# Two attentions: the second half's scores in two pieces, with that half's value rows between them

## The chip, the cores and the metric

One core of a Trainium2 chip. The metric is the device time of one execution in microseconds (us), lower is better. PE is the matmul engine (TensorE), PEld its weight loads, DVE is VectorE, ACT is ScalarE, POOL is GpSimd, SP the engine that issues most DMAs.

## The reference, cut to what matters

A chain of small blocks on x of shape (32, 32, 256): an attention (with a layer norm ahead of it and biases), two gated feed-forward blocks, a second attention (no biases), a linear attention, a paged attention and a mixture of experts. The change touches only the two plain attentions. Each has 16 heads of size 16 over sequences of 32 tokens:

```python
Q, K, V = split_heads(Xn @ Wq + bq), split_heads(Xn @ Wk + bk), split_heads(Xn @ Wv + bv)
scores = jnp.einsum('bhqd,bhkd->bhqk', Q, K) / jnp.sqrt(jnp.float32(D_HEAD))
scores = jnp.where(causal, scores, jnp.float32(-jnp.inf))
A = jax.nn.softmax(scores, axis=-1)
AV = jnp.einsum('bhqk,bhkd->bhqd', A, V)
return AV.swapaxes(-2, -3).reshape(X.shape[:-1] + (D_MODEL,)) @ Wo + bo
```

The second attention scales q by a temperature of its sequence and has no biases; otherwise it is the same.

## The kernel before, in words

Both attentions are one class, `Attention`, called as `att_a` and `att_b` (L1817, L1818). Every engine runs its own list of instructions in the order in which the code writes them; semaphores order the engines against each other, through `wait(engine, name, count)` and `then_inc`. There is no planner: the order of the calls is the schedule.

The 1024 tokens are 8 tiles of 128 (four sequences each), in two halves of four tiles. The 256 features are two chunks (c) of 128. PSUM, where matmuls write, has eight banks, `ps[:, 0..7]`.

PE (`tensor`, L358 to L440), in this order: keys of the first half into banks 0 and 1, queries into 2 and 3 (`project`, L361), value rows of the first half into banks 4 and 5 (`value_rows`, L368, 16 matmuls), then `scores(0)` into banks 0 to 3 (L377): 256 matmuls of 32x32 by 32x64. Then the second half's keys into banks 6 and 7, its queries into 4 and 5, its value rows into 6 and 7 (after `k_kept_late`), and `scores(1)` into banks 4 to 7, which therefore waits until the queries (`q_kept`) and the values (`v_kept`) have been copied out. After the wait for `scaled` 4 (DVE has read all first-half scores) come the weighted sums, `weigh(g)` for the 8 tiles in banks 0 and 1 (L397), with the output projections `out_rows` in banks 2 and 3 (L407) between them.

DVE (`vector`, L442): keys of the first half to SBUF (L450 or L453), the values (`keep_values`, L465 with bias, L469 without), and for each tile `up_to_exponent` (L480 scales and masks the scores out of PSUM, L485 takes the maximum), `sums` (L491, L493) and `turn` (L497, transposes the probabilities). ACT (`scalar`, L532): queries (L538), second-half keys (L545), `exponent` (L552), `place` (L560, three copies of a quarter into a block-diagonal tile), `keep_output` (L565). POOL (`gpsimd`, L590): subtracts the maximum (L599), multiplies by the reciprocal sum (L604), places the last quarter (L612).

For one tile the data goes PE, DVE, POOL, ACT, DVE, POOL, DVE, ACT and POOL, PE. In DVE's list the second half begins at `if g == 4` (L515): `keep_values(2)`, `keep_values(3)`, `sums(3)`, `turn(2)`, `up_to_exponent(4)`. In ACT's list `exponent(4)` stands ahead of `keep_output(0)` and `place(2)`.

Of the kernel before, what the change touches and what calls it, by code (L numbers as in the profile page):

```python
# [33 lines left out]
B, S, D = 32, 32, 256  # L34
T = B * S
KC = D // P
# [175 lines left out]
def program(nc, small_at, x_tok_d, x_feat_d, mix_table, small_d, ints_d, wA_d, wB_d, wF_d, wG_d, wL_d, wP_d,  # L212
# [7 lines left out]
    with ExitStack() as ctx:  # L220
# [87 lines left out]
        def split_buf(name, base, at, cols):  # L308
# [19 lines left out]
              for name, at in (("z_hi", 6656), ("z_lo", 0))]  # L328
# [4 lines left out]
                         max_done=NT, shifted=NT, exp_done=NT, sum_done=NT, rec_done=NT, normed=NT, turned=NT, placed=3 * NT,  # L333
                         placed_last=NT, pv_done=NT, o_kept=NT, proj_done=4, out=4)

        class Attention:


# [12 lines left out]
            def s(self, name):  # L351
                return sem("att_" + name)
# [5 lines left out]
            def tensor(self, pe):  # L358
                s, inp = self.s, self.inp

                def project(w, n, banks, done):  # L361
                    for c in range(KC):
                        for k in range(KC):
                            mm = nc.tensor.matmul(ps[:, banks[c], :], w[:, k, c * P:(c + 1) * P],
                                                  inp[:, k, n * HALF:(n + 1) * HALF], start=(k == 0), stop=(k == KC - 1))
                        mm.then_inc(s(done), 1)

                def value_rows(n):  # L368
                    for g in range(4 * n, 4 * n + 4):
                        for k in range(KC):  # L370
                            mm = nc.tensor.matmul(ps[:, 4 + g // 2, (g % 2) * D:(g % 2 + 1) * D],
                                                  inp[:, k, g * P:(g + 1) * P], self.wv[:, k, :],
                                                  start=(k == 0), stop=(k == KC - 1))
                        if g % 2:
                            mm.then_inc(s("v_done"), 1)

                def scores(n):  # L377
                    for g4 in range(4):
                        for c in range(KC):
                            for pr in range(4):  # L380
                                for j in range(4):
                                    t0 = (4 * (4 * n + g4) + j) * S
                                    mm = nc.tensor.matmul(
                                        ps[32 * j:32 * j + 32, 4 * n + pr, (2 * g4 + c) * 64:(2 * g4 + c + 1) * 64],
                                        qT[32 * pr:32 * pr + 32, c, t0:t0 + S], kpar[32 * pr:32 * pr + 32, c, :, t0:t0 + S],
                                        start=True, stop=True)
                    mm.then_inc(s("scores_done"), 1)

                def weigh(g):
                    self.wait(pe, "placed", 3 * (g + 1))  # L390
                    self.wait(pe, "placed_last", g + 1)
                    if g >= 2:
                        self.wait(pe, "o_kept", g - 1)
                    for c in range(KC):
                        for pr in range(4):
                            for a in range(2):
                                mm = nc.tensor.matmul(ps[32 * pr:32 * pr + 32, g % 2, c * P:(c + 1) * P],  # L397
                                                      vpar[:, g, a, 4 * c + pr, :], pdiag[:, g % 2, 4 * pr + 2 * c + a, :],
                                                      start=(a == 0), stop=(a == 1))
                    mm.then_inc(s("pv_done"), 1)  # L400

                def out_rows(n, c):
                    self.wait(pe, "o_kept", 4 * (n + 1))
                    if n:
                        self.wait(pe, "out", c + 1)
                    for k in range(KC):
                        mm = nc.tensor.matmul(ps[:, 2 + c, :], self.wo[:, k, c * P:(c + 1) * P],  # L407
                                              attT[:, k, n * HALF:(n + 1) * HALF], start=(k == 0), stop=(k == KC - 1))
                    mm.then_inc(s("proj_done"), 1)

                pe.wait_ge(sem(self.load[0]), self.load[1])
                pe.wait_ge(sem(self.in_ready[0]), self.in_ready[1] + 2)
                project(self.wk, 0, (0, 1), "k_done")
                if self.second_input:
                    self.second_input()
                pe.wait_ge(sem(self.in_ready[0]), self.in_ready[1] + 4)
                project(self.wq, 0, (2, 3), "q_done")
                value_rows(0)
                self.wait(pe, "k_kept", 4)
                self.wait(pe, "q_kept", 2)  # L420
                scores(0)
                project(self.wk, 1, (6, 7), "k_done")
                self.wait(pe, "v_kept", 4)
                project(self.wq, 1, (4, 5), "q_done")
                self.wait(pe, "k_kept_late", 4)
                value_rows(1)
                self.wait(pe, "q_kept", 4)
                self.wait(pe, "v_kept", 8)
                scores(1)
                self.wait(pe, "scaled", 4)  # L430
                for g in range(4):
                    weigh(g)
                weigh(4)
                out_rows(0, 0)
                weigh(5)
                out_rows(0, 1)
                weigh(6)
                weigh(7)
                out_rows(1, 0)
                out_rows(1, 1)  # L440

            def vector(self, dve):  # L442
# [14 lines left out]

                def keep_values(i):
                    self.wait(dve, "v_done", i + 1)
                    v = ps[:, 4 + i, :].rearrange("p (g h a d) -> p g h a d", g=2, h=8, a=2)  # L460
                    bv = const("bv").rearrange("p (h a d) -> p h a d", h=8, a=2)
                    for a in range(2):
                        if self.biased:
                            for g in range(2):
                                ins = nc.vector.tensor_tensor(vpar[:, 2 * i + g, a, :, a * HD:(a + 1) * HD],  # L465
                                                              v[:, g, :, a, :], bv[:, :, a, :], ALU.add)
                            ins.then_inc(s("v_kept"), 1)
                        else:
                            nc.vector.tensor_copy(vpar[:, 2 * i:2 * i + 2, a, :, a * HD:(a + 1) * HD],  # L469
                                                  v[:, :, :, a, :]).then_inc(s("v_kept"), 1)  # L470
# [42 lines left out]
                keep_values(1)  # L513
                for g in range(NT + 1):
                    if g == 4:  # L515
                        keep_values(2)
                        keep_values(3)
                        sums(3)
                        turn(2)
                        up_to_exponent(4)  # L520
                        continue
                    if g < NT:
# [1599 lines left out]
```

## Time and profile before

| | |
|---|---|
| three runs | 604.6 us median (602.22, 604.6, 605.16) |
| profiled execution | 608.92 us, its span 607.0 us, mean granted clock 0.882 |
| PE busy | 500.5 us (82%) |
| PE weight loads | 365.2 us (60%) |
| DVE busy | 374.6 us (62%) |
| ACT busy | 235.9 us (39%) |
| POOL busy | 262.3 us (43%) |
| the first attention | about 19 to 84 us of the span |
| the second attention | about 268 to 323 us of the span |

The span runs from the first to the last instruction of one execution. A row of a timeline shows when a run of equal instructions started, how long the run took, and in brackets how long the engine had been idle before it and what ended that; "issue" there is idle time with no cause in the profile. A busy share is an average over stages with different limits, so the stretches around the two score groups have to be read by themselves.

### The profile page before, as it was taken

The numbers are of one execution on the slowest core, as the hardware profiler recorded it, in microseconds if no ns is written. First come the engines' busy times: TensorE is split into PE (matmuls) and PEld (weight loads), VectorE is DVE, ScalarE is ACT, GpSimd is POOL, SyncE is SP. The second block draws the span as 40 slices with busy tenths as digits, with TensorE's granted clock in tenths as the row PEclk, the third lists the DMA queues.
The fourth block names the chain that finished last, engine by engine and source line by source line (L and its number), as shares of the span: only waits on it lengthen the run. The fifth ranks groups of instructions, "written<-read, shape, count | busy, mean of one in ns | idle before, by whom it ended". The sixth has DMA issues, their size and how long they took to land. (4 is left out here: it accounts for less than half of the span.)

```text
span 607.0 us, 10570 instructions
## 1 busy us (share of the span) xinstructions
PE 500.5 (82%) x4069; PEld 365.2 (60%) x4069; DVE 374.6 (62%) x784; ACT 235.9 (39%) x510; POOL 262.3 (43%) x240
## 2 busy tenths in 40 slices
PE   2968699999999999999687599739999894079966
PEld 0545457887687788766553254626776484069956
DVE  3645757887687788855654764976888356124421
ACT  6125855344342443233581001545666241024430
POOL 5023833464353577774550000278860104616650
PEclk9879699999999999999879759958999776569987
DMA  4991027000000122230001919411100001298416
GB/s 164 384 411 50 1 85 188 0 1 1 1 0 1 35 62 60 65 110 3 2 2 35 207 36 351 168 35 27 27 19 2 2 1 44 96 335 274 139 57 206
DMA packets 25969, 55.95 MB, mean 92 GB/s; under 512 B 4744, under 2 KB 17185, under 8 KB 25024
## 3 DMA queue, kind: packets, MB, share of 16 engines
q1 hardware_dynamic: 19952, 45.06, 22.3%
q0 software_dynamic: 5968, 10.22, 5.6%
q8 instruction: 33, 0.54, 0.4%
q14 instruction: 16, 0.13, 0.1%
HBM read 44.24 MB, written 12.37 MB: 93 GB/s over the span
## 5 line engine op out<-in xcount | busy, mean ns | idle before, releaser
L697 PE MATMUL ps<-x_split,gate_up_split 128*128 128x512 f32 x384 | 96.3, 393 | 0.1
L697 PEld LDWEIGHTS ps<-x_split,gate_up_split 128*128 128x128 f32 x384 | 72.0, 188 | 17.1 <-issue 1.4
L1859 POOL DMA_INDIRECT wbig<-new_kv,prepi x40 | 43.4, 1086 | 86.5 <-DMA new_kv<-work 75.4
L890 POOL TENSOR_TENSOR gate_up_split<-wbig,gate_up_split 128x768 fp32r<-128x768 f32 (+1 forms) x24 | 41.6, 1734 | 52.0 <-ACT gate_up_split L830 51.9
L812 DVE TENSOR_TENSOR hidden_split<-work,hidden_split 128x512 fp32r<-128x512 f32 x34 | 37.7, 1110 | 23.1 <-ACT hidden_split L879 23.1
L879 ACT ACTIVATE hidden_split<-work 128x512 fp32r<-128x512 f32 x34 | 21.4, 630 | 61.4 <-DVE work L807 59.2
L721 PE MATMUL ps<-hidden_split,down_split 128*128 128x512 f32 x160 | 42.5, 395 | 3.0 <-issue 1.4
L1804 POOL DMA_INDIRECT chosen<-work,wbig x31 | 30.5, 985 | 29.7 <-issue 15.0
L896 POOL TENSOR_TENSOR down_split<-wbig,down_split 128x384 fp32r<-128x384 f32 (+1 forms) x24 | 29.1, 1214 | 26.2 <-ACT down_split L837 26.1
L599 POOL TENSOR_TENSOR work<-work,prep 128x512 f32<-128x512 f32 x16 | 16.8, 1048 | 53.5 <-DVE prep L485 52.8
L1859 POOL DMA_INDIRECT wbig<-in_cache_dram,prepi x32 | 33.5, 1047 | 7.6 <-issue 6.6
L721 PEld LDWEIGHTS ps<-hidden_split,down_split 128*128 128x128 f32 x160 | 29.8, 188 | 11.0 <-issue 4.6
L1513 ACT ACTIVATE wmid<-ps,prep 128x160 f32<-128x160 f32 x64 | 24.6, 390 | 22.1 <-DVE prep L1412 22.1
L397 PE MATMUL ps<-work 128*32 128x128 f32 x512 | 23.8, 349 | 9.3 <-ACT work L560 9.3
L1801 POOL DMA_INDIRECT sorted<-work,prepi x16 | 16.2, 1013 | 35.1 <-DVE prepi L1671 30.5
L807 DVE TENSOR_TENSOR work<-ps,work 128x512 f32<-128x512 f32 x34 | 23.2, 683 | 12.1 <-PE ps L702 8.5
L560 ACT ACTIVATE work<-work 32x512 f32<-32x512 f32 x48 | 29.9, 624 | 0.9
L872 ACT ACTIVATE work<-ps 128x512 f32<-128x512 f32 x34 | 20.2, 594 | 25.3 <-PE ps L702 13.3
L1707 PE MATMUL ps<-small,wbig 128*128 128x128 f32 x62 | 12.4, 287 | 20.5 <-DMA wbig<-sorted 20.5
L397 PEld LDWEIGHTS ps<-work 128*32 128x32 f32 x512 | 19.0, 136 | 16.1 <-ACT work L560 15.6
L1330 PE MATMUL ps<-work 128*128 128x160 f32 x128 | 27.8, 343 | 0.0
L1782 ACT ACTIVATE work<-ps 128x128 f32<-128x128 f32 x31 | 8.6, 278 | 46.9 <-PE ps L1718 46.9
(321 smaller groups left out, 1162.8 us busy)
## 6 DMA issues: line engine op xcount, KB each, us to landing
work<-in_wE_dram SPq DMA_DIRECT2D x1, 5376.0 KB, 16.1
wbig<-in_wF_dram SPq DMA_DIRECT2D x1, 4992.0 KB, 21.4
work<-work SPq DMA_DIRECT2D x32, 128.0 KB, 2.4
sorted<-wmid SPq DMA_DIRECT2D x1, 3999.0 KB, 15.8
wbig<-in_wG_dram SPq DMA_DIRECT2D x1, 3072.0 KB, 28.2
wbig<-in_wE_dram SPq DMA_DIRECT2D x6, 384.0 KB, 3.8
wbig<-chosen SPq DMA_DIRECT2D x8, 256.0 KB, 5.1
wbig<-sorted SPq DMA_DIRECT2D x1, 1935.0 KB, 13.2
```

The lines of the kernel that those rows point to most:

```text
L397: mm = nc.tensor.matmul(ps[32 * pr:32 * pr + 32, g % 2, c * P:(c + 1) * P], vpar[:, g, a, 4 * c + pr, :], pdiag[:, g % 2, 4 * pr + 2 * c + ...
L560: nc.scalar.activation(pdiag[q, g % 2, :, q], scor[q, g % 4, :].rearrange("p (h k) -> p h k", h=NH), ACT.Copy).then_inc(s("placed"), 1)
L697: mm = nc.tensor.matmul(o, self.gus[:, w % 2, a, 2 * m + k, :], self.xs[:, b, k, n * HALF:(n + 1) * HALF], start=(k == 0 and a == b), stop ...
L721: nc.tensor.matmul(o, self.dns[:, w % 2, a, c], hs[:, i % 2, 0, :], start=(p == 0 and a == 0), stop=False)
L807: nc.vector.tensor_tensor(hid[:, i % 3, :], ps[:, 5 + 2 * (i % 2), :], gated[:, i % 2, :], ALU.mult).then_inc(s("h_ready"), 1)
L812: nc.vector.tensor_tensor(hs[:, i % 2, 1, :], hid[:, i % 3, :], hs[:, i % 2, 0, :].bitcast(F32), ALU.subtract).then_inc(s("h_lo"), 1)
L890: nc.gpsimd.tensor_tensor(self.gus[:, k % 2, 1, 0:self.gu_chunks], self.gate_up[:, :, j * P:(j + 1) * P], self.gus[:, k % 2, 0, 0:self.gu_ ...
L896: nc.gpsimd.tensor_tensor(self.dns[:, k % 2, 1, 0:self.dn_cols], self.down[:, j, :], self.dns[:, k % 2, 0, 0:self.dn_cols].bitcast(F32), A ...
L1330: mm = nc.tensor.matmul(ps[:, 2 + b % 2, a * NKEY:(a + 1) * NKEY], qmask[:, b, 2 * a:2 * a + 2, :, :].rearrange("p g h t -> p (g h t)"), k ...
L1513: nc.scalar.activation(pex[:, b % 3, a, :], ps[:, 2 + b % 2, a * NKEY:(a + 1) * NKEY], ACT.Exp, bias=pst[:, b, a:a + 1], accum_out=pst[:, ...
L1804: send(chosen_d, by(tile_x(t)[:, D + 1:ROW]), y_tile[:, t % 8, :], None, bounds_check=2 * T - 1, oob_is_err=False)\
L1859: return nc.gpsimd.indirect_dma_start(dst, None, table, bass.IndirectOffsetOnAxis(ap=rows.bitcast(U32), axis=0), **({} if bound is None el ...
```

## The change

`value_rows` takes its bank from a tuple: 4 and 5 for the first half as before, 2 and 3 for the second half instead of 6 and 7. `scores` can do one of the two feature chunks alone. On PE the second half's scores of chunk 0 come first, then the wait for `scaled` 4, the value rows, and the scores of chunk 1, which signal `scores_done`. The wait for `v_kept` 8 moves to after the fourth `weigh`. On DVE `sums(3)` and `turn(2)` go ahead of `keep_values(2)` and `keep_values(3)`. The number of instructions stays the same on each engine.

```diff
--- before.py
+++ after.py
@@ -333,6 +333,8 @@
                          max_done=NT, shifted=NT, exp_done=NT, sum_done=NT, rec_done=NT, normed=NT, turned=NT, placed=3 * NT,
                          placed_last=NT, pv_done=NT, o_kept=NT, proj_done=4, out=4)
 
+        VALUE_BANK = (4, 5, 2, 3)
+
         class Attention:
 
 
@@ -368,15 +370,15 @@
                 def value_rows(n):
                     for g in range(4 * n, 4 * n + 4):
                         for k in range(KC):
-                            mm = nc.tensor.matmul(ps[:, 4 + g // 2, (g % 2) * D:(g % 2 + 1) * D],
+                            mm = nc.tensor.matmul(ps[:, VALUE_BANK[g // 2], (g % 2) * D:(g % 2 + 1) * D],
                                                   inp[:, k, g * P:(g + 1) * P], self.wv[:, k, :],
                                                   start=(k == 0), stop=(k == KC - 1))
                         if g % 2:
                             mm.then_inc(s("v_done"), 1)
 
-                def scores(n):
+                def scores(n, chunks=range(KC)):
                     for g4 in range(4):
-                        for c in range(KC):
+                        for c in chunks:
                             for pr in range(4):
                                 for j in range(4):
                                     t0 = (4 * (4 * n + g4) + j) * S
@@ -384,7 +386,8 @@
                                         ps[32 * j:32 * j + 32, 4 * n + pr, (2 * g4 + c) * 64:(2 * g4 + c + 1) * 64],
                                         qT[32 * pr:32 * pr + 32, c, t0:t0 + S], kpar[32 * pr:32 * pr + 32, c, :, t0:t0 + S],
                                         start=True, stop=True)
-                    mm.then_inc(s("scores_done"), 1)
+                    if KC - 1 in chunks:
+                        mm.then_inc(s("scores_done"), 1)
 
                 def weigh(g):
                     self.wait(pe, "placed", 3 * (g + 1))
@@ -423,13 +426,14 @@
                 self.wait(pe, "v_kept", 4)
                 project(self.wq, 1, (4, 5), "q_done")
                 self.wait(pe, "k_kept_late", 4)
+                self.wait(pe, "q_kept", 4)
+                scores(1, (0,))
+                self.wait(pe, "scaled", 4)
                 value_rows(1)
-                self.wait(pe, "q_kept", 4)
-                self.wait(pe, "v_kept", 8)
-                scores(1)
-                self.wait(pe, "scaled", 4)
+                scores(1, (1,))
                 for g in range(4):
                     weigh(g)
+                self.wait(pe, "v_kept", 8)
                 weigh(4)
                 out_rows(0, 0)
                 weigh(5)
@@ -457,7 +461,7 @@
 
                 def keep_values(i):
                     self.wait(dve, "v_done", i + 1)
-                    v = ps[:, 4 + i, :].rearrange("p (g h a d) -> p g h a d", g=2, h=8, a=2)
+                    v = ps[:, VALUE_BANK[i], :].rearrange("p (g h a d) -> p g h a d", g=2, h=8, a=2)
                     bv = const("bv").rearrange("p (h a d) -> p h a d", h=8, a=2)
                     for a in range(2):
                         if self.biased:
@@ -513,10 +517,10 @@
                 keep_values(1)
                 for g in range(NT + 1):
                     if g == 4:
+                        sums(3)
+                        turn(2)
                         keep_values(2)
                         keep_values(3)
-                        sums(3)
-                        turn(2)
                         up_to_exponent(4)
                         continue
                     if g < NT:
```

## Rows read from the trace of the kernel before

**Rows 1.** Timeline, PE, first attention: start us, length us, engine, line, names, count [idle before]
```profile
29.04 3.62 PE L371 MATMUL ps<-wmid,work 128*128 128x256 f32 x16
...
32.59 2.50 PE L383 MATMUL ps<-work 32*32 32x64 f32 x237
...
39.70 0.48 PE L383 MATMUL ps<-work 32*32 32x64 f32 x19 [4.60 <-issue]
...
49.90 3.62 PE L371 MATMUL ps<-wmid,work 128*128 128x256 f32 x16
...
54.58 2.18 PE L383 MATMUL ps<-work 32*32 32x64 f32 x205 [1.06 <-DVE work L465]
...
58.55 0.74 PE L383 MATMUL ps<-work 32*32 32x64 f32 x51 [1.78 <-issue]
```

**Rows 2.** Timeline, DVE and ACT, first attention, around the second half's scores
```profile
47.39 0.65 DVE L480 SCALAR_TENSOR_TENSOR work<-ps,small 128x512 f32<-128x512 f32 x1
...
50.10 0.69 ACT L538 ACTIVATE work<-ps,small 128x512 f32<-128x512 f32 x1 [0.89 <-PE ps L364]
...
53.55 0.88 DVE L465 TENSOR_TENSOR work<-ps,small 128x128 f32<-128x128 f32 x4 [0.84 <-PE ps L371]
54.35 0.67 DVE L491 TENSOR_REDUCE prep<-work 128x16 f32<-128x512 f32 x1
...
55.23 0.65 DVE L497 STREAM_TRANSPOSE work<-work 128x512 f32<-128x512 f32 x1
...
59.33 0.69 DVE L480 SCALAR_TENSOR_TENSOR work<-ps,small 128x512 f32<-128x512 f32 x1 [3.44 <-PE ps L383]
```

**Rows 3.** Timeline, PE, second attention
```profile
278.72 2.71 PE L383 MATMUL ps<-work 32*32 32x64 f32 x256
...
288.33 3.62 PE L371 MATMUL ps<-wmid,xT 128*128 128x256 f32 x16
292.89 2.46 PE L383 MATMUL ps<-work 32*32 32x64 f32 x233 [0.94 <-DVE work L469]
297.18 0.37 PE L383 MATMUL ps<-work 32*32 32x64 f32 x23 [1.83 <-issue]
```

**Rows 4.** Timelines of DVE and of ACT, second attention
```profile
288.47 0.71 DVE L480 SCALAR_TENSOR_TENSOR work<-ps,prep,small 128x512 f32<-128x512 f32 x1
...
297.69 0.75 DVE L480 SCALAR_TENSOR_TENSOR work<-ps,prep,small 128x512 f32<-128x512 f32 x1 [3.49 <-PE ps L383]
...
288.80 1.07 ACT L538 ACTIVATE work<-ps 128x512 f32<-128x512 f32 x2
```

**Rows 5.** Timeline of ACT, first attention, exponent of tile 4
```profile
61.97 0.63 ACT L552 ACTIVATE work<-work 128x512 f32<-128x512 f32 x1 [6.89 <-POOL work L599]
```

**Rows 6.** Windows: stretch, length, busy us of each engine, granted clock, DMA share, GB/s
```profile
32.50:40.20 7.70, 3.10 (x258) 2.65 (x257) 0.88 (x4) 0.00 (x0) 0.00 (x0) 0.92 0.98 417
66.40:76.50 10.10, 7.99 (x77) 4.55 (x80) 6.53 (x13) 8.73 (x16) 7.12 (x9) 0.50 0.00 0
```

**Rows 7.** The page: busy us and instructions by engine; DMA queues (packets, MB, share)
```profile
PE 500.5 (82%) x4069; PEld 365.2 (60%) x4069; DVE 374.6 (62%) x784; ACT 235.9 (39%) x510; POOL 262.3 (43%) x240
...
q8 instruction: 33, 0.54, 0.4%
```

**Rows 8.** DMA in windows (40 slices each): 54.5:59.3, then 292.8:297.6, then 50:54.5
```profile
GB/s 0 0 0 0 0 0 0 0 0 0 0 0 0 137 0 0 0 0 0 0 0 0 0 0 0 0 0 0 0 0 0 0 0 0 0 0 0 0 0 0
...
GB/s 0 0 0 0 0 0 0 0 0 0 0 0 0 0 0 0 137 0 0 0 0 0 0 0 0 0 0 0 0 0 0 0 0 0 0 0 0 0 0 0
...
DMA packets 0, 0.00 MB, mean 0 GB/s; under 512 B 0, under 2 KB 0, under 8 KB 0
```

**Rows 9.** Timeline, PE: output projections, two of the first attention, one of the second
```profile
72.36 3.78 PE L407 MATMUL ps<-work,wmid 128*128 128x512 f32 x4
...
77.33 1.98 PE L407 MATMUL ps<-work,wmid 128*128 128x512 f32 x4
...
310.77 2.61 PE L407 MATMUL ps<-work,wmid 128*128 128x512 f32 x4
```

## The prediction

> **What bounds the kernel now.** I read the page first: in a span of 607.0 us PE is the busiest engine with 500.5 [rows 7], but the two attentions are stretches in which it stands still between bursts. So the timeline of each attention comes next, then the waits of the instructions around the scores, then the DMA of those few microseconds, and last the granted clock.
>
> In both attentions the second half's scores end late. In the first attention PE does the value rows from 49.90, waits until DVE has copied them out (53.55 + 0.88 = 54.43), and starts the 256 score matmuls at 54.58. It gets 205 of them out by 56.8, stands still, resumes at 58.55 and ends at 59.29 [rows 1]. DVE takes the first score tile at 59.33 after 3.44 us of idleness [rows 2]. The second attention repeats it: value rows from 288.33, 0.94 us idle until DVE's copies, scores from 292.89, 233 matmuls, a stop until 297.18, DVE on at 297.69 [rows 3, 4]. After that come shift (POOL), exponent and placing (ACT), weighted sum (PE). ACT's exponent of tile 4 waits 6.89 us for POOL, which waits for DVE [rows 5]; from there on ACT is nearly full (8.73 of 10.1 us [rows 6]) and sets the pace of the tiles, so what the scores end later, the attention ends later, one for one.
>
> The stop inside the scores is no wait of the program; the rows call it "issue". I take it for instruction fetch. The instruction queue q8 moved 33 packets, 0.54 MB in all, 16 KB each [rows 7]. PE has 4069 matmuls and as many weight loads, about 8430 instructions with its waits, so 33 packets hold 256 each, 128 pairs of matmul and weight load. The places fit: from the stop after 237 pairs of the first scores to the stop after 205 of the second are 19 + 16 + 16 + 205 = 256 pairs, two packets. And within each stop's window the only packet on any queue is one of q8 (the one packet of the rows, 0.02 MB): 13 slices of 0.12 us into 54.5 to 59.3, so at 56.1, and 16 slices into 292.8 to 297.6, so at 294.7 [rows 8]. Runs of 237 and 51 pairs take 2.50 and 0.74 us [rows 1], so 9.5 ns a pair and 0.25 us for the last one's own length: a packet is used up in 1.2 us. The packet before the stop's place is entered 77 pairs into the scores (54.58 + 0.73 = 55.3) and the next one can run at 58.55: 3.2 us. The second attention gives 105 pairs, 293.9, to 297.18: 3.3 us. So with 3.3 us between two such borders nothing stops.
>
> **The change part by part.** Times are those of the profiled run (608.92 us, of which the span is 607.0; the median of the runs shown is 604.6, 4.3 lower, and I take differences over to it unscaled).
>
> *Order on PE.* New: wait for q_kept, 128 score pairs (chunk 0), wait for scaled, 16 value matmuls, 128 score pairs (chunk 1). No instruction is added or taken away.
>
> First attention: the last query chunk leaves ACT at 50.10 + 0.69 = 50.79 [rows 2]. Releasing PE took 0.15 before (54.43 to 54.58), so 50.94. 128 pairs at 9.5 ns: 52.15. Value rows take 3.55 from their first matmul to the first score (29.04 to 32.59) [rows 1]: 55.70. 128 pairs and the last one's 0.25: 57.16. DVE begins 0.04 later, 57.20 instead of 59.33: **2.1 us**.
>
> Second: queries leave ACT at 288.80 + 1.07 = 289.87, PE 290.01, then 291.22, 294.77, 296.23; DVE 0.14 later (as 297.55 to 297.69), 296.37 instead of 297.69 [rows 4]: **1.3 us**. It gains less since ACT gives the queries later, 1.5 us behind the value rows' old start.
>
> *Why the stop goes.* The borders lie 93 pairs into the first piece and 77 into the second (121 and 105 in the second attention). Between them are 35 + 77 pairs and the value rows: 1.1 + 3.55 = 4.6 us, over the 3.3 needed, 1.3 to spare. The spare could be eaten by other transfers: the first scores of the first attention, with DMA 98% busy at 417 GB/s, stopped for 4.60 us [rows 1, 6]. From 50 to 54.5, where the first piece will ask for its packet, no packet of any kind moved [rows 8], so I take no delay. Bounds: 0 to 1.3 of stop again in the first attention.
>
> *The new wait, scaled 4,* stands ahead of value rows and behind it are they, the second piece and the weighted sums. DVE finished that read at 47.39 + 0.65 = 48.04, 4.1 us before PE comes at 52.15 [rows 2]; in the second attention at 288.47 + 0.71 = 289.18, 2.0 us before 291.22 [rows 4]. Nothing.
>
> *DVE's order.* sums(3) and turn(2) go ahead of the copies. They took DVE 1.53 us, 54.35 to 55.88, the moment it was free [rows 2], and can now begin earlier. The two pairs of copies take 0.88 each, and the last follows the last value row at 55.70, so DVE is done at 56.6 while PE does the second piece to 57.16. At worst sums begins no earlier than before: 55.88, 56.76, 57.64, and DVE's tile is 0.4 late. I take 0, since the value it waits for is an exponent issued long before; bound 0 to 0.4 in each. PE's wait for v_kept comes after four weighted sums, far later.
>
> *Banks 2 and 3.* They held the first scores, free after scaled 4; out_rows uses them after v_kept 8. No new wait.
>
> *Two more changes of matmul shape in each attention.* Scores start at 32.59, while the value rows' last ends at 29.04 + 3.62 = 32.66 [rows 1]: a switch shows nothing. I take 0. Upper bound: one score matmul's length, 0.25, for each of four switches, 1.0 us in all; nothing could make a switch a gain.
> The Trainium skill (TensorEngine Tiling (Array Packing), Key Properties) says that a change of tiling mode drains the engine. It gives no price; by it the sum would lose something at each switch, and the row above doesn't show it.
>
> *Granted clock.* The tail of the first attention ran at a granted clock of 0.50 (1.2 GHz) from 66.4 to 76.5, behind weighted sums with gaps between them, and so four projection matmuls took 3.78 us against 1.98 right behind; in the second attention the same four took 2.61 [rows 6, 9]. The tails differ by where the fall ends, which the change moves. Worth for each tail: minus 1.8 to plus 1.8 us. I take 0, since the bursts behind the scores keep their spacing, and the fall comes with them.
>
> Sum: 2.1 + 1.3 = 3.4 us, 604.6 - 3.4 = **601.2 us**. What is late next is the query copy on ACT (PE idle 0.7 and 1.4 us ahead of the first piece) and then the chain of DVE, POOL and ACT. Everything later in the kernel starts behind the attentions; the loads of the next weights are landed or triggered by that work, so the gain should reach the end.
>
> **Rivals.**
> *A, the stop stays.* If the stop isn't fetch but belongs to a run of small matmuls, or comes back in the second piece, 2.0 us return in each attention (58.55 less 54.58 + 1.95): 3.4 - 4.0 = -0.6, 605.2 us. For it: the rows name no cause. Against: 256 score pairs ran from 278.72 in 2.71 us without a stop [rows 3], and the places fit borders of 256 instructions. Had 12 pairs moved them to one side, a border lies nearly at that run's start, so its fetch was ahead.
> The Trainium skill (Runtime: NRT & Kernel Launch, Instruction fetch mechanics) has the same 16 KiB blocks of 256 instructions, but calls their cost mostly hidden and gives PE room for 2048 instructions. By that no stop would be fetch, and A would hold; the trace shows a packet of q8 inside the stops, and disagrees.
>
> *B, the clock takes it back.* PE now idles before the first piece and the whole second half comes elsewhere against the clock. If the second attention's tail runs at half clock as the first one's did (3.78 against its 2.61 for four matmuls, 1.2 us, and as much again on the sums and projections behind them) 2.4 us are lost: 603.6 us. For it: two attentions with the same code show two tails. Against: it can as well go the other way.
>
> *C, the other side: each piece stops at its own border.* Every piece contains one border. If a packet is asked for only when PE gets near it, and not while the value rows are waited for, both pieces stop for 2.0 us: -0.6 - 4.0 = -4.6, 609.2 us, slower. It decides where the fetch takes longer than the time between borders, that is above 4.6 us; the stop of 4.60 us at 35 to 39.7 under heavy loads shows that such a time occurs. Against: from 50 on nothing is loading.
>
> **How the numbers follow.** Forecast 0.64, A 0.15, B 0.14, C 0.07. The forecast's own range is 599.0 to 602.8 (clock tails, shape switches 1.0, DVE cover). The range that holds 8 in 10 must reach into A: 598.6 to 605.6. I count over 0.5% (3.0 us, below 601.6) as faster, about what can be told from no change: the forecast lies only 0.4 beyond, so of its 0.64 two thirds are faster, 0.43, and 0.01 of B; slower are C and 0.02 of B, where both tails lose, 0.09; same is the rest, 0.47.
>
> **What would show it.** In the changed kernel's timeline: score matmuls in runs of 128 with no "issue" stop; the first piece right behind ACT's second L538; DVE's first L480 of the second half 6.4 us after the last queries leave ACT in the first attention (57.2 - 50.8) and 6.5 in the second (296.4 - 289.9); q8 packets still one per 256 PE instructions. Wrong if a stop of about 2 us stands in either piece (A, C), if DVE's L465 ends after the last score, if scaled holds PE, or if the gain is there at 60 us and at 300 us but not at the end (B, or a load that waits for nothing of this).

## The result: slower by 0.9%, and the profile after

The changed kernel took 609.4 us (median of 6 runs, 607.33 to 610.49) against 603.6 us (median of 6); the ratio is 1.0093, 95% interval 1.0064 to 1.0122, so 5.6 us slower where 601.2 was forecast. One of the six runs of the kernel before, at 695.58 us, was in a slow state and is left out of the ratio. On another chip the ratio was 1.0119 (1.0075 to 1.0163).

The profiled execution of the changed kernel (607.33 us, span 605.5) was the fastest of its six; that of the kernel before (608.92 us) lay above the 601.5 to 605.2 of its other timed runs. Their spans can't be set against each other; stretches of them can. The timeline of PE, first attention after the change (answers to [rows 1]):

```profile
29.68 3.62 PE L373 MATMUL ps<-wmid,work 128*128 128x256 f32 x16
33.23 2.51 PE L385 MATMUL ps<-work 32*32 32x64 f32 x237
40.71 0.48 PE L385 MATMUL ps<-work 32*32 32x64 f32 x19 [4.97 <-issue]
41.12 8.52 PE L366 MATMUL ps<-work,wmid 128*128 128x512 f32 x16
50.51 1.12 PE L385 MATMUL ps<-work 32*32 32x64 f32 x93 [0.87 <-ACT work L542]
53.81 0.61 PE L385 MATMUL ps<-work 32*32 32x64 f32 x35 [2.18 <-issue]
54.35 5.31 PE L373 MATMUL ps<-wmid,work 128*128 128x256 f32 x16
59.59 1.48 PE L385 MATMUL ps<-work 32*32 32x64 f32 x128
```

and the second (to [rows 3]):

```profile
280.38 2.71 PE L385 MATMUL ps<-work 32*32 32x64 f32 x256
283.03 7.13 PE L366 MATMUL ps<-xT,wmid 128*128 128x512 f32 x16
291.67 1.40 PE L385 MATMUL ps<-work 32*32 32x64 f32 x120 [1.51 <-ACT work L542]
295.64 0.43 PE L385 MATMUL ps<-work 32*32 32x64 f32 x8 [2.57 <-issue]
296.01 5.65 PE L373 MATMUL ps<-wmid,xT 128*128 128x256 f32 x16
301.59 1.47 PE L385 MATMUL ps<-work 32*32 32x64 f32 x128
```

The stop has left the second piece and now stands in the first, at 93 and 120 pairs, the places that the prediction gave for the border there. And the value rows behind it take 5.3 and 5.65 us, not 3.62. DVE, around the second piece (to [rows 2] and [rows 4]):

```profile
59.70 0.89 DVE L469 TENSOR_TENSOR work<-ps,small 128x128 f32<-128x128 f32 x4 [0.84 <-PE ps L373]
61.10 0.69 DVE L484 SCALAR_TENSOR_TENSOR work<-ps,small 128x512 f32<-128x512 f32 x1 [0.52 <-PE ps L385]
```
```profile
301.70 0.76 DVE L473 COPY work<-ps 128x256 f32<-128x256 f32 x2 [1.11 <-PE ps L373]
303.10 0.75 DVE L484 SCALAR_TENSOR_TENSOR work<-ps,prep,small 128x512 f32<-128x512 f32 x1 [0.65 <-PE ps L385]
```

The copies end before the last score, and DVE then waits for PE, as forecast. The windows over the stops and over the value rows (columns as in [rows 6]):

```profile
52.00:53.80 1.80, 0.00 (x0) 0.00 (x0) 0.90 (x3) 1.75 (x4) 0.54 (x1) 1.00 0.00 0
54.40:59.60 5.20, 5.20 (x19) 4.06 (x18) 0.89 (x5) 0.26 (x1) 0.00 (x0) 0.69 0.01 3
293.10:295.60 2.50, 0.00 (x0) 0.00 (x0) 1.51 (x3) 2.43 (x5) 1.28 (x2) 0.50 0.02 7
296.00:301.60 5.60, 5.60 (x22) 4.35 (x18) 0.76 (x2) 0.00 (x0) 0.00 (x0) 0.65 0.01 3
```

PE does nothing in the stops, and the value rows get a mean granted clock of 0.69 and 0.65, a mix of the two levels, 1.2 and 2.4 GHz. The two stops differ: in the first attention the clock is still full during the stop (1.00) and falls behind it, in the second it is at half (0.50) from the stop's start.

Where did the packet come? DMA from 41.5 to 49 us before the change, then after it; then 50 to 54 after it:

```profile
DMA packets 471, 2.34 MB, mean 312 GB/s; under 512 B 192, under 2 KB 192, under 8 KB 320
## 3 DMA queue, kind: packets, MB, share of 16 engines
q1 hardware_dynamic: 470, 2.33, 75.8%
q8 instruction: 1, 0.02, 0.9%
```
```profile
DMA packets 469, 2.30 MB, mean 307 GB/s; under 512 B 192, under 2 KB 192, under 8 KB 320
## 3 DMA queue, kind: packets, MB, share of 16 engines
q1 hardware_dynamic: 469, 2.30, 74.6%
...
GB/s 0 0 0 0 0 0 0 0 0 0 0 0 0 0 164 0 0 0 0 0 0 0 0 0 0 0 0 0 0 0 0 0 0 0 0 0 0 0 0 0
```

Before, one packet of q8 came while PE did the second half's projections (the trace has it at 43.5). After, none did; it came in slice 14 of 0.1 us from 50, at 51.5, 1.0 us after q_kept released PE at 50.45. In the second attention it moved from 284.7 (PE in the query projection) to 293.25, 1.6 us after the release at 291.6. So the packet that the first piece needs started late, with nothing else on the DMA queues.

### The profile page after: what moved, and what is told of

The parts are those of the page before. It is cut to its first block and busy times, and to the rows that moved or that the text cites. A ratio compares the mean times of both kernels' runs of the same rounds, so it can differ in the third digit from the quotient of the medians.

```text
span 605.5 us, 10572 instructions
## 1 busy us (share of the span) xinstructions
PE 498.0 (82%) x4069; PEld 365.1 (60%) x4069; DVE 375.3 (62%) x784; ACT 235.8 (39%) x510; POOL 262.3 (43%) x240
## 5 line engine op out<-in xcount | busy, mean ns | idle before, releaser
L894 POOL TENSOR_TENSOR gate_up_split<-wbig,gate_up_split 128x768 fp32r<-128x768 f32 (+1 forms) x24 | 41.5, 1732 | 51.9 <-ACT gate_up_split L834 51.8
L400 PE MATMUL ps<-work 128*32 128x128 f32 x512 | 20.7, 315 | 12.4 <-ACT work L564 12.4
L400 PEld LDWEIGHTS ps<-work 128*32 128x32 f32 x512 | 16.7, 124 | 19.2 <-ACT work L564 16.1
```

What stands on the lines that cost most here:

```text
L894: nc.gpsimd.tensor_tensor(self.gus[:, k % 2, 1, 0:self.gu_chunks], self.gate_up[:, :, j * P:(j + 1) * P], self.gus[:, k % 2, 0, 0:self.gu_ ...
```

## The experiments

The chips of the groups differ (the kernel before took 618.2, 617.6, 602.5 and 603.3 us there), so ratios to the kernel before on the same chip are compared. "Theory F" is the late fetch: a packet of instructions that is asked for too late. A pair is one weight load and its matmul, and a wait record is an instruction that does nothing but wait.

The instruction stream shows what could hold the request. Where PE waits for two semaphores in a row, the first is carried by the next weight load, and the other becomes a wait record of its own ahead of it. Before the change k_kept_late was carried by the value rows' first weight load. After it, k_kept_late and q_kept stand together, and the trace has a wait record on q_kept at 50.4 and at 291.6 us (`wait` is a helper, L358, so its records have that line; windows 40:60 and 285:300):

```profile
L358 PEldq EVENT_SEMAPHORE  x1: 51/51/51, 50.4 to 50.4; - x1
L358 PEldq EVENT_SEMAPHORE  x1: 51/51/51, 291.6 to 291.6; - x1
```

**e1: one wait.**
```diff
-                self.wait(pe, "k_kept_late", 4)
                 self.wait(pe, "q_kept", 4)
                 scores(1, (0,))
```


> The changed kernel without PE's wait for k_kept_late 4 ahead of the first piece (q_kept 4, which ACT signals later in its order, stays). Theory F (late fetch): of two waits in a row one becomes a wait record of its own in PE's instruction stream, and while PE's sequencer stands in it, behind the first scores, the request for the next instruction packet doesn't go out; the packets come at 51.6 and 293.35 us of the changed trace, 1.1 and 1.7 us behind the release by q_kept. With one wait, carried by the first weight load, the sequencer goes on: packets as early as before the change (43.5 and 284.7 there), no stop at 93 and 120 pairs, value rows at full clock (3.6 us, not 5.3 and 5.65). Time: changed kernel 609.4 less 2 x 2.4 (stops) less 2 x 1.8 (clock) = 601.0. Rival S (spacing: two dense pieces are too close behind the first scores for the fetch, whatever the waits): both stops stay at 2 to 3 us, 609.4. Rival K (the loss is made by the clock alone): the stops stay or go without moving the time by more than 1 us.

Ratio 0.9947 (0.9914 to 0.9980), where 601.0 us, that is 0.9957, was expected. PE in the second series (e1_again):

```profile
50.33 1.48 PE L385 MATMUL ps<-work 32*32 32x64 f32 x128 [0.78 <-ACT work L541]
51.74 3.72 PE L373 MATMUL ps<-wmid,work 128*128 128x256 f32 x16
55.39 1.48 PE L385 MATMUL ps<-work 32*32 32x64 f32 x128
...
286.14 1.48 PE L385 MATMUL ps<-work 32*32 32x64 f32 x128 [1.42 <-ACT work L541]
287.54 3.72 PE L373 MATMUL ps<-wmid,xT 128*128 128x256 f32 x16
291.19 1.48 PE L385 MATMUL ps<-work 32*32 32x64 f32 x128
```

Whole pieces, no stop, value rows at full clock. The packets came at 45.6 and 282.4 in e1_one_wait, while PE did the projections. S and K are out: same matmuls, same spacing, one wait record less in each attention, no stops, and 1.5% between this and the changed kernel. The two ratios are from different chips; on one chip, below, the changed kernel (1.0119) and two versions without its stops in the second halves (e6 0.9993, e7 0.9978) are 1.3 and 1.4% apart.

**e2: the two waits in the other order.**
```diff
-                self.wait(pe, "k_kept_late", 4)
                 self.wait(pe, "q_kept", 4)
+                self.wait(pe, "k_kept_late", 4)
                 scores(1, (0,))
```


> The changed kernel with the two waits ahead of the first piece in the other order, so that the wait of its own is k_kept_late (released at 47.8 us in the first attention, about 289.3 in the second) and q_kept (50.4 and 291.5) is carried by the weight load. Theory F: the packets are asked for some 1.1 to 1.7 us behind the release of the wait of its own, so they move from 51.6 to about 49.2 and from 293.35 to about 290.7, and each stop shrinks from 2.2 and 2.6 us to 0 to 0.7; time 601 to 604. Rival S: nothing changes, 609.4, since the instructions and their number are the same.

0.9915 (0.9883 to 0.9947). The packets came at 49.18 and 285.60, each 1.1 to 1.2 us behind the end of ACT's second-half keys (48.05 and 284.36), the release of the wait record; no stop, the first pieces 1.70 and 1.59 us long instead of 1.48. (This profile reaches the second attention's first scores 4.9 us earlier than the changed kernel's, 275.4 against 280.4, so 285.6 stands for the 290.7 expected.) The packet follows the wait record.

**e3: the kernel before, with q_kept's wait moved ahead of the value rows.**
```diff
                 self.wait(pe, "k_kept_late", 4)
-                value_rows(1)
                 self.wait(pe, "q_kept", 4)
+                value_rows(1)
```


> The kernel before with one line moved: PE waits for q_kept 4 together with k_kept_late 4 ahead of the value rows; nothing is split, banks as before. Theory F: the packets that came at 43.5 and 284.7 come 1.1 to 1.7 us behind q_kept's release, at about 52 and 291.5, and the value rows begin 0.9 and 1.5 us later; the stops inside the scores keep their place (205 and 233 pairs), and a further stop at 77 and 105 pairs comes only if packet plus 2.2 us is later than that: 54.2 against 56.2, so none. Time 603.6 + 2.4 = 606.0 or less. Rival S: packets where they were, time 606 as well; the packets' times tell the two apart, not the total.

1.0047 (1.0013 to 1.0080), 2.9 us. The packets came at 54.2 and 294.3, 1.0 and 1.6 us behind the record's release (53.17 and 292.68), and the stops kept their places (205 and 233 pairs). So without any split the same wait record holds the packet back. DMA of e3 from 44 to 56 us, slices of 0.3:
```profile
GB/s 382 437 437 367 389 447 391 393 468 262 151 117 113 44 56 26 0 0 0 0 0 0 0 0 0 0 0 0 0 0 0 0 0 0 55 0 0 0 0 0
```

**e4: borders moved by 20 pairs.** `for j in [0] * (10 if g == 0 else 0) + list(range(4)):` in the first gather's matmuls.

> The changed kernel with ten surplus 32x32 matmuls (20 pairs of matmul and weight load, 40 instructions) behind the first gather, where PE waits for the next gather anyway; they write again what is written there. If the stops are borders of instruction packets of 256, all stops move 20 pairs ahead: the first scores' from 237 to 217 pairs, the first pieces' from 93 to 73 and from 120 to 100. If they belong to runs of small matmuls or to the data, they stay at 237, 93 and 120. The time may change little: 609 plus up to 1.

PE in e4:
```profile
37.96 2.34 PE L385 MATMUL ps<-work 32*32 32x64 f32 x217
...
55.45 1.47 PE L385 MATMUL ps<-work 32*32 32x64 f32 x128 [0.87 <-ACT work L542]
...
294.40 1.19 PE L385 MATMUL ps<-work 32*32 32x64 f32 x100 [0.78 <-ACT work L542]
297.72 0.39 PE L385 MATMUL ps<-work 32*32 32x64 f32 x28 [2.14 <-issue]
```
237 became 217 and 120 became 100: the stops are borders of the stream. The one expected at 73 didn't come. Its packet came at 47.0 us. I read that so: with the border 40 instructions earlier, it had been asked for before the sequencer reached the wait record. That I had not foreseen. In the second attention the borders moved by 40 instructions too, and there the packet was late all the same, at 295.39, 1.05 us after the record's release at 294.34. The second attention's first scores, free of stops before, stopped at 245 pairs. Ratio 1.0132 of two runs; the surplus matmuls at the start weren't hidden as expected (the second key block starts at 30.87, in the other profiles at 25.5 to 28.2), so its total says nothing.

**after_again: the changed kernel beside the next three.**

> The changed kernel unaltered, on the chip of this group, so that the others can be set against it. If theory F holds in all: first pieces of 93 and 120 pairs, a stop, value rows of 5.3 to 5.7 us, and a ratio to the kernel before near 1.009. If the ratio of 1.009 came from anything outside the attentions, it may be elsewhere here.

1.0119; 93 and 120 pairs, stops of 2.17 and 2.30 us, value rows of 5.41 and 5.85. The packets came 1.04 and 1.16 us after the record's release.

**e5: no split.** Banks 2 and 3, DVE's new order and the late v_kept wait kept, `scores(1)` whole behind the value rows.

> The changed banks and the later v_kept wait alone: value rows of the second half in banks 2 and 3 (after scaled 4) first, then all 256 score pairs in one piece (q_kept carried, k_kept_late as the wait of its own). The scores needn't wait for the copies of the values: PE goes on at 49.90 + 3.55 = 53.45 instead of 54.58, and at 291.88 instead of 292.89, 2.1 us in all; the stops at 205 and 233 pairs stay, 2.0 us each. Time: before less 2.1 us, ratio 0.9965. If the value of the split is that the fetch gets time between borders, this stays behind the split kernels of one wait (0.9947 and 0.9915) by the stops less the wait for the queries, about 1.3 us. If it is as fast or faster, the split brought nothing.

0.9973 (0.9956 to 0.9991), 1.7 us faster than before where 2.1 were expected. Stops of 1.91 and 1.92 us at 205 and 232 pairs. Against the split without its stops (0.9947 and 0.9915 in the group before, 0.9981, 0.9963 and 0.9971 below) the difference is not resolved: no total here shows that the split itself gains anything over e5. e5 too has a wait record (on k_kept_late, at 50.5 and 288.7), but its value rows stand between the border and the record, and its packets came before it, at 44.8 and 284.0.

**e6: DVE's old order on e1.**

> The changed kernel without the k_kept_late wait (as e1_one_wait) and with DVE's old order: keep_values(2), keep_values(3), sums(3), turn(2). The last copies can't begin before the last value row, and sums and turn (1.5 us) now follow them, while the second score piece takes 1.5: DVE reaches the second half's first tile about 1.0 us late in each attention. Expected ratio to the kernel before 0.9947 + 0.0033 = 0.998. If DVE's order is worth nothing, 0.995 as e1.

0.9993 (0.9965 to 1.0021), where e1 had 0.9947 (on another chip; 0.9981 and 0.9963 later, so the totals don't resolve it). DVE in e6, then in e1_again:
```profile
56.35 0.89 DVE L468 TENSOR_TENSOR work<-ps,small 128x128 f32<-128x128 f32 x4 [0.84 <-PE ps L373]
57.15 0.68 DVE L494 TENSOR_REDUCE prep<-work 128x16 f32<-128x512 f32 x1
57.87 0.25 DVE L496 RECIPROCAL prep<-prep 128x16 f32<-128x16 f32 x1
58.03 0.65 DVE L500 STREAM_TRANSPOSE work<-work 128x512 f32<-128x512 f32 x1
58.61 0.65 DVE L483 SCALAR_TENSOR_TENSOR work<-ps,small 128x512 f32<-128x512 f32 x1
```
```profile
55.49 0.88 DVE L468 TENSOR_TENSOR work<-ps,small 128x128 f32<-128x128 f32 x4 [0.40 <-PE ps L373]
56.90 0.69 DVE L483 SCALAR_TENSOR_TENSOR work<-ps,small 128x512 f32<-128x512 f32 x1 [0.52 <-PE ps L385]
```
In e6 DVE goes straight from the transposition to the scores and starts 0.9 us after the last one (56.24 + 1.47 = 57.71); in e1 it waits for PE. In the second attention e6's DVE starts 0.75 us after the last score (298.20 against 297.45), e1_again's 0.04. The new order is worth 0.9 and 0.7 us at this place.

**e7: the first attention's first half split too, on e2.** `scores(0, (0,))`, `value_rows(0)`, `scores(0, (1,))`.

> The version of e2_waits_swapped with the first half of the first attention split too: chunk 0 of scores(0), value rows, chunk 1. There the stop is 4.4 to 5.3 us, since the fetch takes about 6 us from border to resumption while weights are loading. Borders then lie 125 pairs into the first piece and 109 into the second, 4.6 us apart: the stop shrinks to about 1.5 us. PE waits about 1.1 us for q_kept 2 ahead. Expected 2 to 2.5 us less than e2, ratio 0.987 to 0.989. If the stop there belongs to something else that ends at a fixed time (the weight loads), nothing is gained, or 1 us lost.

0.9978 (0.9951 to 1.0005), no gain where 0.987 to 0.989 was expected. The first piece stopped for 2.85 us at 125 pairs and the value rows took 6.24 at a mean granted clock of 0.58. Its packet came at 32.8, 3.6 us after the release of the wait record on k_kept (29.2), under full DMA load. I read it as the same mistake made anew, but did not try it without the record, and the load alone may have made the packet late. In the second half of that attention e7 has e2's two waits and a wait record released at 49.6, but the packet came at 46.15, ahead of it. The instructions are the same there; what differs is that PE had passed the border before it without a stop (e2 stopped there for 4.42 us). So a record so close behind a border does not always hold the packet.

**e8: value rows in two pieces as well.** PE's list (`value_rows` takes the tiles as an argument):
```diff
-                self.wait(pe, "k_kept_late", 4)
-                self.wait(pe, "q_kept", 4)
-                scores(1, (0,))
                 self.wait(pe, "scaled", 4)
-                value_rows(1)
+                value_rows(1, (4, 5))
+                self.wait(pe, "q_kept", 4)
+                scores(1, (0,))
+                value_rows(1, (6, 7))
                 scores(1, (1,))
```


> The changed kernel with the value rows in two pieces as well: 8 value matmuls (tiles 4 and 5, behind scaled 4) ahead of the first score piece, 8 behind it, and k_kept_late's wait dropped, so that no wait record of its own is left. PE fills the wait for the queries: first attention 49.9, 51.7, first piece to 52.9, values to 54.7, second piece to 56.2, against 57.2 before; second attention 289.3 (scaled), 291.1, 292.3, 294.1, 295.6 against 296.2. The borders are 1.22 + 1.78 = 3.0 us apart where 3.3 are needed: a stop of about 0.3 us in each second piece. Sum about 1 us less than e1 and e2, ratio 0.993. Rival: with less than 3.3 us between borders the stops and the clock behind them come back in full (2 us and more each), and it is slower than e1.

1.0008 (0.9991 to 1.0026); and once more:

> e8_values_in_halves once more. Its attentions took 55.2 and 53.9 us in the first profile, 5.8 us less together than the profile of the kernel before, yet its time was that of the kernel before (ratio 1.0008). If the gain within the attentions is real but its total was a matter of that chip or of the clock behind, the ratio here is nearer to 0.995; if something later always gives it back, it is 1.001 again.

0.9992 (0.9969 to 1.0015). The second pieces took 1.62 and 1.52 us (1.72 and 1.53 in the repeat), so the stops were at most 0.2. From the first value row to the last score it took 6.8 us in each attention where 6.3 was expected; the time was that of the kernel before all the same.

**e1 and e2 repeated.**

> e1_one_wait once more, to be set against e2_again and e8 on one chip. Theory F: no stops in the second half's scores, so its ratio lies where the first forecast had the change, 3.4 us under the kernel before, 0.9945.

> e2_waits_swapped once more. Its instructions and e1's differ by one wait record, and both ran without a stop, so they should be equal, near 0.9945; the 0.9915 of the first group was then in part the clock's phase. If the swapped order is really better, it repeats 0.9915.

> e1_one_wait a third time (0.9947, 0.9981 so far). Theory F with the tails' clock phase: the ratio lies between 0.994 and 0.999, without stops; attentions of 55.4 to 56.7 and 55.4 to 57.1 us.

e1: 0.9981 (0.9941 to 1.0022) and 0.9963 (0.9923 to 1.0002). e2: 0.9971 (0.9934 to 1.0008). In e2_again's second attention the value rows took 5.41 us without any stop ahead:

```profile
287.00 1.59 PE L385 MATMUL ps<-work 32*32 32x64 f32 x128 [1.42 <-ACT work L542]
288.52 5.41 PE L373 MATMUL ps<-wmid,xT 128*128 128x256 f32 x16
```
```profile
288.50:293.80 5.30, 5.30 (x23) 4.14 (x16) 2.26 (x5) 2.66 (x5) 1.30 (x2) 0.68 0.01 3
```

PE had idled 1.42 us for the queries, and the clock fell 1.7 us after the piece's start. Without a stop ahead the second attention's value rows were slow in two more profiles, e6 (5.41) and e7 (5.22), each behind 1.42 or 1.43 us of idle time, and at 3.72 in the other four (e1 three times, e2), behind the same idle time. In the changed kernel's second attention the clock fell 1.4 us after the piece's start, at 293.1, when the stop had only begun: that fall is not shown to be the stop's doing. In the first attention all eight profiles without a stop in the first piece have value rows of 3.72 us, and the two with one 5.31 and 5.41. e1's twelve runs of that group lie in two bunches: five at 596.96 to 597.19 us with a mean granted clock of 0.90, and five at 604.6 to 605.8 with 0.886 to 0.889.

**Profiles of the kernel before.**

> The kernel before once more, for a second profile. From its first key projection of the second block (L364) to the feed-forward block's first matmul the first attention took 59.8 us, the second 55.1 from its first matmul to the linear attention's. Theory T (the tails' clock phase moves a single attention by up to 1.8 us either way): here 58 to 61 and 54 to 57, the difference lying behind the scores. If both repeat within 0.3 us, what e1 lacks in the second attention (55.4 against 55.1) is the edit's own doing.

The expectation of the third said the same. From the second key block (L364) to the feed-forward block's first matmul, and from the second attention's first matmul to the linear attention's, in us, each from one profile:

```
kernel             first    second   both
before             59.8     55.1     114.9
before, 2nd        58.45    56.9     115.3
before, 3rd        58.4     56.5     114.9
changed            60.8     60.3     121.1
changed, again     61.0     58.7     119.7
e1 (three)    55.9 55.4 55.0   55.4 55.4 53.85   111.3 110.8 108.9
e2 (two)           55.5 56.7    55.5 57.1        111.0 113.8
e8 (two)           55.2 57.4    53.9 54.0        109.1 111.4
```

One attention of the unchanged kernel varies by 1.4 to 1.8 us with the clock of its tail (its four output projections took 2.61, 3.67 and 3.78 us in the second attention). The changed kernel's two are 5.4 us above the mean of before (120.4 against 115.0), nearly all of the 5.6 that the runs show.

The rest of the program varies as well. The stretch from the linear attention's first matmul to the paged attention's first transposition (L1307 of the kernel before), and from there to the next L721, in e1_again, in e8_again, then in before_p2 and before_p3, all on one chip:

```profile
319.85:388.34 68.49, 53.37 (x169) 29.64 (x169) 47.26 (x89) 15.59 (x24) 2.46 (x2) 0.83 0.58 177
388.34:499.31 110.97, 92.36 (x929) 69.59 (x929) 77.54 (x248) 54.07 (x189) 52.74 (x50) 0.84 0.06 15
320.19:390.27 70.08, 54.91 (x168) 29.53 (x168) 47.44 (x89) 15.60 (x24) 2.45 (x2) 0.81 0.57 172
390.27:504.46 114.19, 93.25 (x928) 69.89 (x929) 77.10 (x248) 54.10 (x189) 52.54 (x50) 0.85 0.06 15
325.07:395.14 70.07, 56.44 (x168) 30.53 (x168) 47.34 (x89) 15.59 (x24) 2.45 (x2) 0.77 0.57 172
324.88:393.30 68.42, 55.00 (x169) 30.17 (x169) 47.33 (x89) 15.59 (x24) 2.47 (x2) 0.80 0.59 177
```

The two stretches together take 179.5 us in e1_again, but 183.4 in e1_third, and 184.3 in e8_again (184.2 in e8's first profile); the unchanged kernel shows 183.4 (70.1 and 113.3) and 179.8 (68.4 and 111.4). So both of e8's profiles lie at the slower level there, and e1 and the unchanged kernel have profiles at either. The 4 to 5 us between the levels are as much as the attentions gained.

## Why the prediction was wrong, by its own steps

- *The stop is instruction fetch, its borders lie 256 instructions apart, and 93, 77, 121 and 105 pairs into the pieces.* Right, shown by e4 (a shift of 20 pairs) and by the packets' times. 121 was 120.
- *"Why the stop goes": this step failed.* It compared the time between the two borders inside the pieces (4.6 us) with 3.3 and found no stop; the second pieces indeed had none. It took for granted that the packet for the first border would be there as before the change, since before it was. Its transfer had come while PE's sequencer ran on into the value rows. The changed order put a wait record on q_kept in its way, and it came 1.0 and 1.6 us after the release, into a piece that reaches the border in 0.9 and 1.1 us. e1, e2 and e3 show it from three sides. The prediction said that no instruction was added; the trace has 293 wait records on PE instead of 291, and above all one in each attention stands in another place. It asked who waits behind each new wait, but not what else the sequencer does while it waits.
- *The Trainium skill's sentence* that crossing a 16 KiB border is mostly hidden (Runtime: NRT & Kernel Launch, Instruction fetch mechanics) is not what these runs show: stops of 1.7 to 5.4 us. Its 256 instructions to a block agree with them.
- *Granted clock, taken as 0.* Wrong by 3.5 us: the value rows ran partly at 1.2 GHz. In the first attention (1.6) that comes with the stop; in the second (1.9) the clock had fallen as the stop began, and e2_again and e6 lose 1.7 there with no stop, so how much of it is the stop's stays open. The sum with what was measured, each stretch against the same one of e1_again: first piece to value rows 3.84 against 1.41 us and 4.34 against 1.40, together 5.4; value rows to second piece 5.24 against 3.65 and 5.58 against 3.65, together 3.5. The forecast gain of 3.4, less the 0.6 of the shapes (below), less 8.9, is 6.1 us slower; measured 5.6.
- *Rival C* named the first piece's own border and a request that isn't made while PE waits, and forecast 609.2 us. The time came out within 0.2 us by luck: it had both pieces stop, and no clock. Only the first pieces stopped, and the clock made up the rest. At 0.07 its chance was far too low. *Rival A* is out: no stop in the second piece, none in e1. *Rival B* had the clock as the thief but looked at the tails; it fell on the value rows, and in the second attention B's condition, PE idle before the first piece, is what stood ahead of the fall.
- *Order on PE.* Right: PE started 0.14 us behind ACT's queries, and without the stops (e1_again) DVE's first tile came 6.6 us after they left ACT in both attentions (56.90 - 50.28, 292.71 - 286.08), where 6.4 and 6.5 were forecast.
- *DVE's order, banks, scaled 4.* Right; e6 prices the DVE order at 0.9 and 0.7 us, more than the bound of 0.4, since the alternative there keeps both copies ahead of sums.
- *Shape switches, taken as 0.* Too low, within the bound of 1.0 in all: in e1_again the first value row starts 1.41 us after the first score (forecast 50.94 to 52.15, 1.21) and the second piece 3.65 after the first value row (forecast 3.55), 0.3 in each attention. Among score matmuls the next one starts every 9.5 ns; the first value row starts 0.14 us after the last score, 0.07 before its end. The row that the prediction read (32.59 against 32.66) shows the switch in the other direction.
- *The gain of 3.4 us should reach the end.* Only in part. Without the stops the three e1 series are 3.3, 1.1 and 2.2 us faster than before, while their profiled attentions are 4.7 us shorter on the mean. e8's profiled attentions are as short and its total gains nothing (0.5 us slower and 0.5 faster). In e8's profiles the two stretches behind the second attention take 184 us against 179.5 in e1_again, the linear attention at a granted clock of 0.81 against 0.83, the later stretch at 0.85 against 0.84. That is where it is lost there; what decides between the levels, and whether the edit has a part in it, stays open. The two bunches of e1's runs go with the mean granted clock; no profile of that group is of the slower bunch.

No version here is clearly better than the kernel before by more than 1%; e1 and e2 are the best, 0.2 to 0.9% faster, and two of their five intervals exclude 1. So does that of e5, the version without a split (0.9973).

## What to carry to other kernels

A wait is not only a delay for what stands behind it: a second wait in a row became a record of its own here, and where PE's sequencer reached such a record shortly behind a border, the next packet of instructions mostly came only after the record's release. Before a dense run of small matmuls leave one wait, let a later signal of the same engine stand for an earlier one, and put the wait that is released first last. And where a change removes a stop by spacing borders, check for every border since when its packet can have been asked for, not only the distance to the border before.

## What the runs showed of the hardware

- Where a wait record stood close behind a border of PE's instruction packets, the next packet's transfer began only 1.0 to 1.7 us after the record's release: in the changed kernel, e2 and e3, each attention, and again in after_again, e2_again and in e4's second attention. With a carried wait (before, e1) it began during the projections, 3 to 6 us ahead of the wait's release. Two cases went the other way, e4's first attention (the border 40 instructions further ahead) and e7's (the same distance as in e2, no stop at the border before). How far ahead of the record a border has to lie is not measured.
- PE's granted clock fell behind 1.4 us of idle time and one piece of scores in three profiles (e2_again, e6, e7: value rows of 5.2 to 5.4 us) and not in four of nearly the same code (e1 three times, e2: 3.72), which moved an attention by 1.5 to 1.7 us.
- In the first attention a stop of 2.2 us cost more than itself: the 16 value matmuls behind it took 5.3 to 5.4 us instead of 3.7.
